# Another order of the experts in block 0, with four weight tiles loaded earlier

## The reference

```python
x = layernorm(x + mamba2(x))        # in-projection, causal conv of 4, chunked scan, gate, RMS norm, out-projection
x = layernorm(x + ffn(x))
# ffn: three weights [2048 x 512], each replaced by clip(round(W/s), -1, 1)*s with s = mean(|W|) + 1e-8
#      hidden = silu(x @ wu.T) * (x @ wg.T);   out = hidden @ wd.T
```

## Time and profile before

| | us |
|---|---|
| median of 3 runs | 1472.15 (1471.26 to 1475.18) |
| profiled execution | 1473.74 |
| its span, first to last instruction | 1471.7 |
| PE busy in it | 1447.2 (98%) |
| DVE / ACT / POOL busy | 1016.4 / 861.0 / 432.1 |
| granted clock of PE, mean | 0.995 of full |

### The profile page before, as it was taken

The page is one execution under the profiler, slowest core; times in us unless marked ns, Lnnn a source line. Parts: engine busy times, 40 slices in busy tenths (PEclk is TensorE's granted clock), DMA queues, the critical chain, the costliest instruction groups (busy, mean ns, idle before and its releaser), DMA issues.

```text
span 1471.7 us, 26863 instructions
## 1 busy us (share of the span) xinstructions
PE 1447.2 (98%) x10132; PEld 1303.3 (89%) x10132; DVE 1016.4 (69%) x2219; ACT 861.0 (59%) x1655; POOL 432.1 (29%) x544
## 2 busy tenths in 40 slices
PE   9999999999999999999998999999999999999997
PEld 8889898889898888998976889999999999999996
DVE  6776686667766776678668987766565666666555
ACT  7876667576765676767762234545455454545443
POOL 5334554445435453354362106500000000000001
PEclk9999999999999999999999999999999999999999
DMA  7113312332233232332247333445353545445341
GB/s 272 65 48 97 101 52 80 87 101 84 65 98 87 80 86 55 99 100 59 87 132 255 108 115 123 166 136 167 112 179 101 158 122 165 130 126 169 100 136 66
DMA packets 141760, 168.05 MB, mean 114 GB/s; under 512 B 76480, under 2 KB 85184, under 8 KB 141632
## 3 DMA queue, kind: packets, MB, share of 16 engines
q1 hardware_dynamic: 141632, 166.35, 36.8%
HBM read 132.62 MB, written 33.69 MB: 113 GB/s over the span
## 4 chain that ended last, share of the span: by engine, by line
PE 89%; DMA 4%; DVE 3%; ACT 2%; issue 1%; SPq 1%; POOL 0%; DVEq 0%; ACTq 0%
PE ps L403 25%; PE ps L265 23%; PE ps L473 16%; PE ps L359 11%; PE ps L313 3%; PE ps L393 3%; DMA x_scratch<-s_rr 2%; PE ps L321 2%; PE ps L330 2%; PE ps L300 1%; DVE s_xact L841 1%; SPq L1406 1%; PE ps L233 1%; PE ps L286 1%; DMA s_rr<-in_un 0%
## 5 line engine op out<-in xcount | busy, mean ns | idle before, releaser
L403 PE MATMUL ps<-s_xoh,s_S 128*128 128x256 f32 x896 | 220.3, 281 | 0.1
L403 PE MATMUL ps<-s_xol,s_S 128*128 128x256 f32 x896 | 220.3, 282 | 0.0
L473 PE MATMUL ps<-s_tern,s_hh 128*128 128x512 f32 x504 | 199.2, 395 | 0.0
L473 PE MATMUL ps<-s_tern,s_hl 128*128 128x512 f32 x504 | 199.2, 395 | 0.0
L265 PE MATMUL ps<-s_uhi,s_whi 128*128 128x256 f32 x1088 | 180.7, 288 | 2.7 <-ACT s_uhi L543 2.7
L403 PEld LDWEIGHTS ps<-s_xoh,s_S 128*128 128x128 f32 x896 | 169.5, 189 | 5.9 <-issue 0.9
L265 PE MATMUL ps<-s_uhi,s_wlo 128*128 128x256 f32 x1088 | 174.5, 283 | 0.0
L265 PE MATMUL ps<-s_ulo,s_whi 128*128 128x256 f32 x1088 | 174.1, 282 | 0.0
L403 PEld LDWEIGHTS ps<-s_xol,s_S 128*128 128x128 f32 x896 | 169.4, 189 | 4.8
L1284 POOL TENSOR_TENSOR s_lnb<-s_lnb,s_cst 128x1 f32<-128x1 f32 x32 | 18.2, 572 | 497.0 <-DVE s_lnb L1131 497.0
L403 PE MATMUL ps<-s_xol,s_tern 128*128 128x256 f32 x672 | 163.7, 281 | 0.0
(11 more groups left out here) (182 smaller groups left out, 2986.2 us busy)
## 6 DMA issues: line engine op xcount, KB each, us to landing
s_S<-wsum_scratch SPq DMA_DIRECT2D x48, 512.0 KB, 3.6
s_S<-wsum_scratch SPq DMA_DIRECT2D x96, 256.0 KB, 3.4
s_bcx<-ct_scratch SPq DMA_DIRECT2D x32, 512.0 KB, 3.8
s_wst<-in_wffn SPq DMA_DIRECT2D x48, 256.0 KB, 2.8
s_wraw<-in_wffn SPq DMA_DIRECT2D x16, 768.0 KB, 8.1
...
```

Of the source, the lines that this page charges most:

```text
L403: o = e.matmul(bank[:, 256 * mi:256 * mi + 256], wt(mi, k), xo[g % 2][:, x, k, :], start=(first and mi == 0 and k == 0 and xo is xoh), sto ...
L473: o = e.matmul(DB[c][:], y[:, 128 * c:128 * c + 128], tern[:, j, 1024:1536], start=(j == 0 and lo == 0), stop=(j == 15 and lo == 1))
```

## The change

What is computed stays the same. J0 is a new list: the tile that block 0 takes at each of its 16 places. The tiles 3, 4, 9 and 10 come first; they lie over in-projection weights that the last five ip steps don't use, and their loads wait for ip(15, 4) instead of ip(15, 8). These four loads stand in SP's list inside the last pair of groups. x1h lies over xact, so its making waits for the last TR and for POOL's last write there, no longer for the last ip; x1n0, which shares that place, is loaded only when block 0's gates are done. WT, wtot, scales and the memset for WT move into the last pair of groups. And the calls behind it are in another order on every engine: in PE's, expert(0, 0) comes ahead of OP(30).

```diff
-    x1h, _ = sb("x1h0", [128, 4, 512], F32R, o_u + 8192)
+    x1h, _ = sb("x1h0", [128, 4, 512], F32R, o_xact)
+    J0 = [3, 4, 9, 10, 0, 1, 2, 5, 6, 7, 8, 11, 12, 13, 14, 15]
...
 def SQ(c):
-                if c % 2 == 0:
-                    if c < NCH - 2:
-                        w.wait_ge(s_GM, c // 2 + 2)
-                    else:
-                        w.wait_ge(s_scl, 1)
+                if c % 2 == 0 and c < NCH - 2:
+                    w.wait_ge(s_GM, c // 2 + 2)
+                elif c == NCH - 3:
+                    w.wait_ge(s_scl, 1)
...
 def WT():
-            w.wait_ge(s_ms, NCH - 2)
+            w.wait_ge(s_ms, NCH - 3)
...
 def expert(j, mi):
-   tern[:, j, ...]
+   tern[:, J0[j], ...]          # and so in ternary(j), and in down for block 0
...
 PE, in the last pair of groups
             ip(n + 1, 3); ip(n + 1, 4); ST(c + 2); G(n + 1); ip(n + 1, 5); OP(c + 2); Y(c + 3); SQ(c + 2)
+            if m == NG // 2 - 1:
+                WT()
             ip(n + 1, 6); ip(n + 1, 7); ST(c + 3); TR(c + 4, 1); TR(c + 4, 0); ip(n + 1, 8); TR(c + 5, 0); SQ(c + 3)
...
 PE, c = 30
-        OP(c - 1); WT(); ST(c); Y(c); Y(c + 1); SQ(c); OP(c); expert(0, 0); expert(0, 1); expert(1, 0); expert(1, 1)
-        expert(2, 0); expert(2, 1); OP(c + 1); SQ(c + 1); expert(3, 0); expert(3, 1); expert(4, 0); expert(4, 1)
+        OP(c - 1); ST(c); Y(c); Y(c + 1); SQ(c); expert(0, 0); OP(c); expert(0, 1); expert(1, 0); expert(1, 1)
+        expert(2, 0); expert(2, 1); SQ(c + 1); OP(c + 1); expert(3, 0); expert(3, 1); expert(4, 0); expert(4, 1)
...
 ACT
 def f_x1h(k):
             w.wait_ge(d_xf, 128)
-            w.wait_ge(s_ip, 9 * NG)
+            w.wait_ge(s_TR[0], NCH)
+            w.wait_ge(s_TR[1], NCH)
+            w.wait_ge(s_zero, 5 * NG + 5)
...
-        f_zs(NG - 1, 3); f_E(c + 1); f_xTe(c + 1, 1); f_xTe(c + 1, 0); f_x1h(0); f_ygh(c); f_sq(c); f_x1h(1); f_x1h(2)
-        f_x1h(3); f_sil(0); f_hh(0); f_sil(1); f_ygh(c + 1); f_sq(c + 1); f_sil(2); f_sil(3); f_hh(1); f_hh(2)
+        f_xTe(c + 1, 1); f_zs(NG - 1, 3); f_E(c + 1); f_xTe(c + 1, 0); f_x1h(0); f_x1h(1); f_x1h(2); f_x1h(3); f_sq(c)
+        f_ygh(c); f_sil(0); f_sil(1); f_sq(c + 1); f_ygh(c + 1); f_hh(0); f_sil(2); f_hh(1); f_hh(2); f_sil(3)
...
 DVE, in the last pair of groups
             f_S(c + 2); f_taps(n + 1, 3); f_taps(n + 1, 4); f_x1(c); f_gate(c + 3, 0); f_x1(c + 1); f_gate(c + 3, 1)
+            if m == NG // 2 - 1:
+                wtot()
             f_ms(c + 2); f_dd(c + 4); f_xt(c); f_r1(c + 2); f_sqsum(c + 3); f_xt(c + 1); f_x1(c + 2)
+            if m == NG // 2 - 1:
+                scales()
...
-                f_wz(c + 4); wtot()
+                f_wz(c + 4)
...
 DVE, c = 30
-        f_ms(c - 1); f_M(c + 1); f_gate(c, 0); f_gate(c, 1); f_x1l(0); f_S(c); f_sqsum(c); scales(); f_x1l(1); f_ms(c)
-        f_r1(c - 1); ternary(0); f_x1l(2); f_x1l(3); f_gate(c + 1, 0); f_xt(c - 2); f_gate(c + 1, 1); ternary(1)
-        f_h(0); ternary(2); f_sqsum(c + 1); f_r1(c); f_h(1); f_x1(c - 1); ternary(3); ternary(4); f_hl(0); f_ms(c + 1)
+        f_ms(c - 1); f_M(c + 1); f_gate(c, 0); f_gate(c, 1); f_x1l(0); f_S(c); f_x1l(1); f_x1l(2); f_sqsum(c)
+        f_x1l(3); ternary(0); f_r1(c - 1); ternary(1); f_ms(c); f_x1(c - 1); f_gate(c + 1, 0); f_gate(c + 1, 1)
+        f_xt(c - 2); f_h(0); ternary(2); f_sqsum(c + 1); f_r1(c); f_h(1); ternary(3); f_hl(0); ternary(4); f_ms(c + 1)
...
 POOL: f_ones() moves behind f_rs(26); f_S123 waits for the later of its two tiles in J0's order
 SP
 def load_tern(j):
-            w.wait_ge(s_ip, 9 * NG)
+            if j in J0[:4]:
+                w.wait_ge(s_ip, 9 * NG - 4)
+            else:
+                w.wait_ge(s_ip, 9 * NG)
...
 def load_x1(g), g == 0
-                w.wait_ge(s_TR[0], NCH)
-                w.wait_ge(s_TR[1], NCH)
+                w.wait_ge(s_gt, 16)
...
-            store_x1(c); store_xt(c); store_x1(c + 1); load_wst(3 * n + 6); store_x1(c + 2); store_xt(c + 1)
+            store_x1(c); store_xt(c); store_x1(c + 1)
+            if m == NG // 2 - 1:
+                load_tern(3); load_tern(4); load_tern(9); load_tern(10)
+            load_wst(3 * n + 6); store_x1(c + 2); store_xt(c + 1)
             if m == NG // 2 - 1:
                 load_xt0()
             load_r0(c + 3)
...
-        load_tern(0); load_x1(0); load_tern(1); load_tern(2); load_tern(3); store_xt(c - 2); load_tern(4)
-        load_tern(5); load_r0(c); load_r0(c + 1); load_tern(6); load_tern(7); load_tern(8); load_tern(9)
+        load_tern(0); load_tern(1); load_tern(2); load_r0(c); load_tern(5); store_xt(c - 2); load_r0(c + 1)
+        load_xt(1, 0); load_tern(6); load_tern(7); load_tern(8); store_x1(c - 1); load_xt(1, 1); load_tern(11)
```

More of the change, by code:

```diff
@@ L461, in down @@
                 w.wait_ge(s_tern, 3 * j + 3)
+            wd = tern[:, j if g else J0[j], 1024:1536]
             for c in part:
@@ L502, in program_pe @@
         c = NCH - 2
-        OP(c - 1); WT(); ST(c); Y(c); Y(c + 1); SQ(c); OP(c); expert(0, 0); expert(0, 1); expert(1, 0); expert(1, 1)
-        expert(2, 0); expert(2, 1); OP(c + 1); SQ(c + 1); expert(3, 0); expert(3, 1); expert(4, 0); expert(4, 1)
[L505 to L508, removed]
+        OP(c - 1); ST(c); Y(c); Y(c + 1); SQ(c); expert(0, 0); OP(c); expert(0, 1); expert(1, 0); expert(1, 1)
+        expert(2, 0); expert(2, 1); SQ(c + 1); OP(c + 1); expert(3, 0); expert(3, 1); expert(4, 0); expert(4, 1)
+        down(0); down(1); expert(5, 0); expert(5, 1); down(2); expert(6, 0); expert(6, 1); down(3); expert(7, 0)
+        down(4); expert(7, 1); expert(8, 0); down(5); expert(8, 1); expert(9, 0); down(6); expert(9, 1); expert(10, 0)
+        expert(10, 1); expert(11, 0); expert(11, 1); down(7); expert(12, 0); down(8); expert(12, 1); expert(13, 0)
+        expert(13, 1); down(9); down(10); expert(14, 0); expert(14, 1); expert(15, 0); expert(15, 1); down(11)
         for Q in range(56):
@@ L1007, in ternary @@
         def ternary(j):
-            w.wait_ge(d_w[j], 32)
+            w.wait_ge(d_w[J0[j]], 32)
             w.wait_ge(s_thr, 1)
@@ L1159, in program_dve @@
             if m == NG // 2 - 1:
[L1160 removed]
+                f_wz(c + 4)
         c = NCH - 2
[L1162 to L1169 removed]
+        f_ms(c - 1); f_M(c + 1); f_gate(c, 0); f_gate(c, 1); f_x1l(0); f_S(c); f_x1l(1); f_x1l(2); f_sqsum(c)
+        f_x1l(3); ternary(0); f_r1(c - 1); ternary(1); f_ms(c); f_x1(c - 1); f_gate(c + 1, 0); f_gate(c + 1, 1)
+        f_xt(c - 2); f_h(0); ternary(2); f_sqsum(c + 1); f_r1(c); f_h(1); ternary(3); f_hl(0); ternary(4); f_ms(c + 1)
+        f_hl(1); f_h(2); f_r1(c + 1); f_h(3); ternary(5); f_hl(2); ternary(6); f_h(4); f_hl(3); ternary(7); f_h(5)
+        ternary(8); f_xt(c - 1); f_hl(4); f_x1(c); ternary(9); f_hl(5); f_h(6); f_x1(c + 1); f_h(7); f_hl(6); f_hl(7)
+        f_h(8); ternary(10); f_hl(8); f_xt(c); f_xt(c + 1); ternary(11); f_h(9); ternary(12); f_hl(9); f_h(10)
+        f_xd(1, 0); ternary(13); f_h(11); f_hl(10); ternary(14); f_h(12); f_hl(11); ternary(15); f_tl(1, 0); f_h(13)
+        f_xd(1, 1); f_xl(1, 0); f_hl(12); f_xl(1, 1); f_hl(13); f_h(14); f_tl(1, 1); f_h(15); f_hl(14); f_hl(15)
         for Q in range(56):
@@ L1308, in f_S123 @@
                 w.wait_ge(d_ss, 64 * Q)
-            w.wait_ge(s_tern, 3 * j2 + 3)
+            w.wait_ge(s_tern, 3 * max(J0.index(j1), J0.index(j2)) + 3)
             e.tensor_tensor(S[0], tw(j2, 0), tw(j2, 1), add).then_inc(s_S4, 1)
@@ L1345, in program_pool @@
             if m == NG // 2 - 1:
-                f_Cexp(c + 4); f_xw(c + 4); f_ones()
+                f_Cexp(c + 4); f_xw(c + 4)
         c = NCH - 2
-        f_DI(c); f_DI(c + 1); f_Sd(c); f_rs(c - 1); f_Cexp(c + 1); f_ygl(c); f_rs(c); f_ygl(c + 1); f_rs1(c - 1)
-        f_rs(c + 1); f_rs1(c); f_rs1(c + 1); f_S123(0); f_S4(0)
+        f_DI(c); f_rs(c - 1); f_DI(c + 1); f_Sd(c); f_Cexp(c + 1); f_ygl(c); f_rs1(c - 1); f_rs(c); f_ygl(c + 1)
+        f_rs1(c); f_rs(c + 1); f_rs1(c + 1); f_S123(0); f_S4(0)
         for p in range(7):
```

26 lines of the change are left out of this document (11 added, 15 removed).

## The result

| | before | after |
|---|---|---|
| median, 20 runs each | 1474.76 us | 1479.16 us |
| lowest to highest | 1470.31 to 1477.64 | 1472.95 to 1482.26 |
| profiled execution (span) | 1473.74 (1471.7) | 1474.94 (1472.9) |

The ratio is 1.0033, with a 95% interval of 1.0023 to 1.0043. I had said 1472.2, "no change", with a range up to 1475.8: the change is slower, and the time lies outside the range. Of the 7.0 us between 1472.2 and 1479.16, only 4.4 are the change's. The other 2.6 are the kernel before: its median is 1474.76 over 20 runs, and I had taken it from 3 runs (1472.15).

The account below looks back on a forecast made before the run. PE, busy in 98% of the span, was taken as the bound; +2.05 for WT, of which 0.5 absorbed, +0.85 before the first expert and -2.35 at OP(31) gave +0.05, hence 1472.2 us, range 1468.8 to 1475.8.

Parts of the forecast that it names:

- step 3: Y(30) to the first expert: DVE's queue sums to 8.1 us, expert(0, 0) starts at 780.2, late by 2.25 us.
- step 4: Clock at expert(0, 0) and OP(30): one fall counted once more, 1.8 us; late by 2.35 us after them.
- step 7: The four early weight loads: x1f lands at 770, hidden behind ACT's work; cost 0, upper bound 2.5 us.
- E(3,0): The expert behind OP(31): forecast to start 57.46 us after SQ(28), against 57.41 before.
- Step 1: WT behind SQ(28): PE waits for ms(28), so ip(15, 6) starts 2.05 us later, bounds 0.2 and 2.3.
- Step 2: Start of Y(30): late by 1.5 us, as the old wait for xTe(31) takes 0.5 of WT's delay.
- Step 5: Ahead of OP(31): the wait for r1(30) goes, load_r0(30) being issued earlier; the 2.35 us are given back.
- step 6: From 804.5 on: both lists have done the same work and PE doesn't wait; cost 0, bounds 0 and 2 us.
- x1f comes late: ACT's queue, x1h ahead of sq(30): x1f lands at 775.1, +2.5 us, 1474.7; chance 0.12, with a further stall 0.06.
- the rule on ring order: DMA: on each engine descriptors of one queue are consumed in ring order, so x1f can't overtake the weights.
- Step 8: The remaining moves (x1h's new place, x1n0's later load, POOL's later S123, other reorderings): cost nothing.

Follow-up runs that it names:

- the second trace: A second profiled execution of the changed kernel, nothing altered: 1478.59 us, nearer to what that kernel usually does than the first profiled one.

## Why the prediction was wrong

Three things were missing from the sum: what POOL's instructions do to x1l (step 3), a fall of the clock at the new wait at WT (step 4), and, in the second trace, the late x1f (step 7). And the starting point was 2.6 us too low, as said above. What I had forecast at E(3,0) was 57.46. It came at 58.77 and, in the second trace, at 61.48. Step by step:

- **Step 1** was right: a wait of 1.80 us on ms(28), where I had said 1.9. **Step 2** was nearly right: Y(30) was 1.88 late, not 1.5 (+0.35).
- **Step 3 failed in size.** From Y(30) to the first expert I had 11.4 us (the terms add up to 8.1, so to 780.0, where I wrote 780.2); it was 12.54 (+1.14) and 14.27 (+2.87). The instructions were the right ones in the right order, but I took each at its duration alone. x1l(0) and x1l(3) were held up by POOL in after, by 1.66 + 1.00 - 2 x 0.68 = 1.3 (x1l(0) by POOL's instruction from 773.17 to 774.45, x1l(3) by ygl(30), 776.61 to 779.01). In the second trace x1l(0) waited 1.47 for the late x1h and x1l(3) took 2.03 beside ygl(30) (779.35 to 781.70). With the loads back and ygl behind ternary(0) it was 12.19, of which 1.0 is still x1l(0), at 1.66 beside another instruction of POOL; without that it would be 11.2, near my 11.4.
- **Step 4 failed in what it left out.** I had the clock fall once behind the pause ahead of the expert, for 1.75, so 24.3 us from expert(0,0) to E(3,0). In after that was right: one fall, 24.1. In the second trace the pause was 3.25 us instead of 2.3, the low stretch three times as long, and the way 25.1; without a fall it is 22.7. And I had no fall at all at WT's pause, which came in four of eight traces for 1.5 more. I had looked for falls only where the old trace has one; a new pause is a new place for them.
- **Step 5** went as said (both waits for r1 are gone, and the way to E(3,0) in after is as forecast), and so did **step 6**: PE 72.00 busy of 72.00. But the gain of step 5 could not pay for what the others had left out.
- **Step 7 failed in the second trace, not in after.** I put x1f's landing at 770, and said that it decides from 773 on. In after x1h(0) started at 772.45, just in time: DVE went from the gates to x1l(0) without a pause. In the second trace it started at 27.37 behind SQ(28), which is 774.4 on the clock of before, and x1l(0) waited 1.47. The rival "x1f comes late" had about this landing, but neither the place nor the mechanism. The place is DVE's queue, where x1l(0) waits for x1h(0) and S(30) and all else stand behind it; in ACT's queue, which the rival named, sq(30) was done at 778.32 in this trace, no later than x1l(2) on DVE (778.35). As for the mechanism, I had made the loads compete for bandwidth. From SP's last x1f issue to x1h(0) it is 2.5 us before, 3.0 in after and 3.6 with the loads alone, so most of the lateness is in SP's issues, which start later and take longer. Whether the rule on ring order that I cited in step 7 holds, no run here shows; the forecast didn't fail by it, but by taking SP's issues at their old length. In the changed kernel this cost cannot be added to that of the lock: taking the loads back gained nothing, since x1l came early and met ygl(30).
- **Step 8** holds as far as the runs show.

Put together: 0.35 + 1.14 - 0.18 (the rest) = 1.31 above the forecast in after, 0.35 + 2.87 + 0.80 = 4.02 in the second trace. With a fall at WT in half of the executions, 0.75 on the average, the seam is 4.8 later than in before if the second trace is the usual case; the medians differ by 4.4. That is an account over few traces and not a proof of each term.

What is shown by timed runs: WT's place alone costs 3.4, 3.6 and 4.25 us in the medians of three pairs (2.7, 4.7 and 4.4 by the ratios), so it is the largest single cause. Two further pairs show less, 1.5 and 2.2 (by the ratios 1.8 and 3.4). In the first of them the early loads are still there, and x1h(0) comes at 28.14, too late for an earlier Y(30) to help. For the second I have no reason but the scatter of the runs: the kernels of the 4.25 had the lock just as well. Without WT's place, the early loads and the meeting of ygl(30) with ternary(0) and x1l, the change is worth nothing (0.9999). Two of its new waits, 1.8 ahead of SQ(30) and 2.1 ahead of the expert, stand in for those that it took away, and the clock stays low twice as long as in before (3.4 us for 1.7 in the measure of the table above).

My range had a flaw of its own. Its upper end, 1475.8, lies only 1.0 above the median of the kernel before over 20 runs: it was laid around a median of three, with the bound of one term on top, though several of the terms can fail at once.

**Still open.** The loads alone put the seam 3.0 us back in both traces of that kernel, but the medians rose by only 0.7 and 2.1 (intervals of the ratio from 0.9991 to 1.0024); whether these are usual executions I can't tell. What decides in an execution whether the clock falls at a pause of 1.8 us isn't known, nor what makes the start of SQ(28) scatter between 744.7 and 751.0.
